# GpSimd's tap sums on VectorE, and another order of steps at the two ends of the attention

## The reference

```python
n = layernorm(x)                               # per token, 1024 channels
c = conv1d(n, conv_w, width 3) + conv_b        # 1024 -> 768 = q | k | v, 256 each
# blocks of 128 tokens, 16 heads of 64, causal inside a block
qh, kh, vh = q@wq + bq, k@wk + bk, v@wv + bv
p = softmax(where(causal, qh @ kh.T / 8, -1e9))
o = (p @ vh) @ wo + bo                         # 1024 -> 256
x1 = x + o @ proj_w + proj_b                   # 256 -> 1024
f = layernorm(x1)
y = f @ W_base.T + b_base                      # 1024 -> 1024
# 4 active experts of rank 8, gate = softmax(log prior + router logits)
out = x1 + y + sum_e 2 * gate_e * (f @ A_e.T) @ B_e.T
```

## Time and profile before

| | |
|---|---|
| median of 3 runs | 793.99 us (793.89 to 794.37) |
| the profiled execution | 794.1 us, of which 792.3 from the first to the last instruction |
| mean granted TensorE clock | 0.997 |
| TensorE busy | 767.2 us (97%) |
| VectorE busy | 516.3 us (65%) |
| ScalarE busy | 384.1 us (48%) |
| GpSimd busy | 203.1 us (26%) |

### The profile page before, as it was taken

How to read it: one execution, slowest core, us unless ns; L and a number is a source line. 1 busy time by engine, 2 the same in 40 slices (tenths; PEclk the granted TensorE clock), 3 DMA queues, 4 the chain that set the end, 5 groups by cost and what they waited for, 6 DMA issues and landing times.

```text
span 792.3 us, 14391 instructions
## 1 busy us (share of the span) xinstructions
PE 767.2 (97%) x5182; PEld 693.0 (87%) x5182; DVE 516.3 (65%) x1478; ACT 384.1 (48%) x1052; POOL 203.1 (26%) x192
## 2 busy tenths in 40 slices
PE   4999999999999999999999999999999999999996
PEld 3898888778778889989999989999889999999996
DVE  6999994778878756444444445545686766667652
ACT  5953442334333887676767676767851101111010
POOL 2400102222222235253534334352401111111100
PEclk9999999999999999999999999999999999999998
DMA  8746834534446230403063332102253534435301
GB/s 327 283 133 165 269 104 148 182 116 148 140 165 239 87 122 1 141 8 109 40 233 127 99 111 90 59 29 81 91 151 133 160 108 132 144 96 160 102 33 54
DMA packets 49435, 101.39 MB, mean 128 GB/s; under 512 B 10195, under 2 KB 26451, under 8 KB 48084
## 3 DMA queue, kind: packets, MB, share of 16 engines
q1 hardware_dynamic: 47060, 92.08, 35.3%
q0 software_dynamic: 2304, 8.39, 2.6%
HBM read 73.97 MB, written 26.08 MB: 126 GB/s over the span
## 4 chain that ended last, share of the span: by engine, by line
PE 69%; DVE 20%; ACT 5%; issue 2%; POOL 2%; DMA 0%; DVEq 0%; ACTq 0%; POOLq 0%
PE net_psum L63 17%; PE net_psum L65 17%; PE net_psum L64 17%; PE net_psum L1389 4%; PE net_psum L1412 4%; PE net_psum L1400 4%; DVE x_lo L950 2%; PE net_psum L1442 2%; PE net_psum L1443 2%; PE net_psum L1444 2%; POOL raw L520 1%; DVE raw L957 1%; ACT pr L682 1%; DVE ua L912 1%; DVE raw L958 1%
## 5 line engine op out<-in xcount | busy, mean ns | idle before, releaser
L63 PE MATMUL net_psum<-fw_hi,xT_hi 128*128 128x354 f32 (+1 forms) x384 | 127.2, 331 | 0.4 <-DVE fw_lo L1191 0.4
L64 PE MATMUL net_psum<-fw_lo,xT_hi 128*128 128x354 f32 (+1 forms) x384 | 124.2, 324 | 0.0
L65 PE MATMUL net_psum<-fw_hi,xT_lo 128*128 128x354 f32 (+1 forms) x384 | 124.2, 323 | 0.0
L546 POOL TENSOR_TENSOR pr<-pr,rrec 128x512 f32<-128x512 f32 x64 | 68.5, 1071 | 207.2 <-DVE rrec L1029 204.2
L682 ACT ACTIVATE pr<-pr,negmax 128x128 f32<-128x128 f32 x256 | 99.1, 395 | 1.0 <-DVE negmax L1021 1.0
L1327 PE MATMUL net_psum<-ua,wa 128*128 128x256 f32 x384 | 83.8, 379 | 0.5 <-DVE ua L915 0.5
L1021 DVE CUSTOM_DVE_ANT_0 pr<-net_psum,mask 128x128 f32<-128x128 f32 x256 | 57.1, 286 | 37.7 <-PE net_psum L1389 37.4
L1327 PEld LDWEIGHTS net_psum<-ua,wa 128*128 128x128 f32 x384 | 72.6, 190 | 10.3 <-issue 0.7
L63 PE MATMUL net_psum<-x_hi,w_hi 128*128 128x512 f32 x192 | 76.7, 400 | 1.7 <-DVE w_lo L964 1.5
L520 POOL TENSOR_TENSOR raw<-raw 128x512 f32<-128x512 f32 x24 | 36.8, 1536 | 161.2 <-ACT raw L631 161.2
L64 PE MATMUL net_psum<-x_lo,w_hi 128*128 128x512 f32 x192 | 76.0, 396 | 0.0
(11 more groups left out here) (191 smaller groups left out, 1813.9 us busy)
## 6 DMA issues: line engine op xcount, KB each, us to landing
wa<-in_conv_w SPq DMA_DIRECT2D x24, 512.0 KB, 4.0
raw<-in_conv_w SPq DMA_DIRECT2D x24, 384.0 KB, 3.8
xn<-in_x SPq DMA_DIRECT2D x16, 512.0 KB, 10.4
xr<-in_x SPq DMA_DIRECT2D x8, 1024.0 KB, 5.0
x_scratch<-xr SPq DMA_DIRECT2D x8, 1024.0 KB, 4.3
x1t<-x_scratch SPq DMA_DIRECT2D x16, 512.0 KB, 3.9
out<-y POOLq DMA_DIRECT2D x16, 512.0 KB, 4.9
x1g<-x_scratch SPq DMA_DIRECT2D x56, 128.0 KB, 3.2
```

Of the source, the lines that this page charges most:

```text
L63: pe.matmul(out, w_hi, x_hi, start=first, stop=False)
L64: pe.matmul(out, w_hi, x_lo, start=False, stop=False)
L65: return pe.matmul(out, w_lo, x_hi, start=False, stop=last)
L546: pool.tensor_tensor(pr[:, jj % 4], pr[:, jj % 4], rrec[:, jj % 4].unsqueeze(2).to_broadcast([P, UN, P]), ALU.mult).then_inc(s["p_ready"], 1)
```

## The change

Seven edits, on VectorE, ScalarE, GpSimd and TensorE:

1. `POOL_SUMS = 2`: GpSimd adds the scaled taps for units 0 and 1 only; for the other 22 VectorE does it, ahead of its two mixes, and waits for pre_ready itself.
2. `ends` of a block moves from the block's second slot to its third, but for the last block but one.
3. `low_weight(0)` goes ahead of the last two low parts of the input.
4. In double steps 2, 3 and 4 the queries and keys of the odd pair are copied out by VectorE (`queries_keys`, new) instead of ScalarE.
5. wo_lo (`low_heads`) goes from the ends of steps 2 and 3 to the end of step 1 and into step 4.
6. In step 32 TensorE's second projection unit goes behind the output sums; on VectorE one fw_lo (`low_dense(3)`) goes behind the masking, and both reciprocals ahead of the second addition.
7. The second half of tile 1's transposes uses bank 3 instead of 7, and waits for the pT copies instead of the last addition to x.

```diff
@@ -104,2 +104,3 @@
     FILL = 18
+    POOL_SUMS = 2
     EARLY = 5
@@ -261,3 +262,3 @@
         gp = psum[:, 0, 0:2 * TG].rearrange("p (g v) -> p g v", g=TG)
-        tp = ((psum[:, 0], psum[:, 6]),) + ((psum[:, 0], psum[:, 7]),)
+        tp = ((psum[:, 0], psum[:, 6]),) + ((psum[:, 0], psum[:, 3]),)
         yp = (tuple(psum[:, b] for b in (1, 2, 4)), tuple(psum[:, b] for b in (5, 6, 3)))
@@ -559,3 +560,3 @@
                 power(1, j)
-            for k in range(NK):
+            for k in range(POOL_SUMS):
                 mix(k)
@@ -735,4 +736,2 @@
                         queries_keys(2 * D)
-                    if D in (2, 3, 4) and h == 1:
-                        queries_keys(2 * D + 1)
                     if pair_of(D - SC) and (D, h) != (ND, 0):
@@ -955,2 +954,5 @@
                 tap = r[:, 0:1].to_broadcast([P, 2, 2, P])
+                if k >= POOL_SUMS:
+                    dve.wait_ge(s["pre_ready"], k + 1)
+                    dve.tensor_tensor(r[:, 2:5:2], r[:, 1:4:2], r[:, 2:5:2], ALU.add).then_inc(s["ef_ready"], 1)
                 dve.wait_ge(s["ef_ready"], k + 1)
@@ -1004,2 +1006,3 @@
                     sums(m, 0, TOK // P).then_inc(s["add_step"], 1)
+                if m >= 0 and k % NP4 == (1 if m == LAST - 1 else 2):
                     dve.wait_ge(s["add_step"], m + 1)
@@ -1043,2 +1046,11 @@
 
+            def queries_keys(J):
+                i = J % NP
+                dve.wait_ge(s["qk_done"], J + 1)
+                wait(dve, s["sc_done"], J - 1)
+                dve.wait_ge(s["qk_ready"], J)
+                for k, t in enumerate((qf, kf)):
+                    c = dve.tensor_scalar(t[:, J % 2], qk_acc(J)[:, k], bqk_c[:, k, i:i + 1], None, ALU.add)
+                c.then_inc(s["qk_ready"], 1)
+
             def unit_out(D, k):
@@ -1083,11 +1095,12 @@
                     low_dense(D - (ND - 3))
-                unit_out(D, 0)
                 if D == ND:
-                    reciprocals(2 * (D - SC))
-                    unit_out(D, 1)
-                    reciprocals(2 * (D - SC) + 1)
-                else:
-                    for jj in pair_of(D - SC):
-                        reciprocals(jj)
-                    unit_out(D, 1)
+                    low_dense(3)
+                if D == 4:
+                    low_heads(1)
+                unit_out(D, 0)
+                if D in (2, 3, 4):
+                    queries_keys(2 * D + 1)
+                for jj in pair_of(D - SC):
+                    reciprocals(jj)
+                unit_out(D, 1)
                 if D == 1:
@@ -1095,8 +1108,5 @@
                     last_sums(2)
+                    low_heads(0)
                 if D == 2:
                     last_sums(3).then_inc(s["cy_ready"], 1)
-                if D in (2, 3):
-                    k = D - 2
-                    dve.wait_ge(s["wo_hi_ready"], k + 1)
-                    dve.tensor_tensor(wo_lo[:, 4 * k:4 * k + 4], wo_raw[:, 4 * k:4 * k + 4], wo_hi[:, 4 * k:4 * k + 4], ALU.subtract).then_inc(s["wo_lo_ready"], 1)
                 if D in (5, 6):
@@ -1105,2 +1115,7 @@
 
+            def low_heads(k):
+                h = slice(4 * k, 4 * k + 4)
+                dve.wait_ge(s["wo_hi_ready"], k + 1)
+                dve.tensor_tensor(wo_lo[:, h], wo_raw[:, h], wo_hi[:, h], ALU.subtract).then_inc(s["wo_lo_ready"], 1)
+
             def tile_statistics(t):
@@ -1225,5 +1240,6 @@
                 inputs(c)
+                if c == DC - 1:
+                    low_weight(0)
                 if c:
                     low_input(c - 1)
-            low_weight(0)
             low_input(DC - 1)
@@ -1258,3 +1274,2 @@
             low_dense(2)
-            low_dense(3)
             attention_pair(ND)
@@ -1464,5 +1479,8 @@
                     queries_keys(2 * D + 1)
-                run_unit(D, 1)
+                if D != ND:
+                    run_unit(D, 1)
                 for jj in pair_of(D - PV):
                     output_sums(jj)
+                if D == ND:
+                    run_unit(D, 1)
 
@@ -1474,3 +1492,3 @@
                     if t == 1 and h == 1:
-                        pe.wait_ge(s["x1_ready"], YT * NG)
+                        pe.wait_ge(s["pT_ready"], NJ)
                     wait(pe, s["xT_lo_ready"], 2 * (t - 1) + h + 1)
```

More of the change, by code:

```diff
@@ L1083, in attention_pair @@
                     low_dense(D - (ND - 3))
+                if D == ND:
+                    low_dense(3)
+                if D == 4:
+                    low_heads(1)
                 unit_out(D, 0)
-                if D == ND:
-                    reciprocals(2 * (D - SC))
-                    unit_out(D, 1)
-                    reciprocals(2 * (D - SC) + 1)
-                else:
-                    for jj in pair_of(D - SC):
-                        reciprocals(jj)
-                    unit_out(D, 1)
+                if D in (2, 3, 4):
[3 more added lines that the diff above has]
+                unit_out(D, 1)
                 if D == 1:
```

## The result

The changed kernel takes 786.35 us (median of 4 runs, 786.11 to 786.48), the kernel before in the runs beside it 794.0 (793.89 to 794.37, 4 runs): a ratio of 0.9904, 95% interval 0.9892 to 0.9916. The forecast was 787.1 in 785.4 to 789.8. The profiled execution took 786.38 with a span of 784.5, against 794.1 and 792.3.

What follows compares the result with a forecast made beforehand. TensorE was taken to set the pace, so moved work counts only through its waits. Convolution 2.5, attention's start 2.3, attention's end 1.7 and last transposes 0.4 sum to 6.9 off 794.1; the median lies 0.1 lower: 787.1 us, range 785.4 to 789.8.

Steps and rivals of the forecast that it cites:

- Convolution: Convolution units: w_lo waits, lost overlap and the late first split matmul all go, for -2.5 us.
- ends go to the next slot: Convolution on VectorE: ends (two steps) leave the slot of the sums, so w_lo no longer comes at the last moment.
- VectorE no longer meets GpSimd: Convolution: w_lo, up to 1.98 against 1.22, and the first of the ends, 1.66 against 0.69, are no longer lengthened.
- The 0.69 a sum: Convolution: a tap sum on VectorE costs 0.69 us, like the mixes, adding some 14 us of VectorE time.
- The 2.7 us of cover: Convolution: the next w_lo is done about 2.9 us into a unit and needed at 5.6, leaving 2.7 spare.
- Rival 4: Convolution: slower because sums on VectorE cost GpSimd's median of 1.6 us, making VectorE the bound; 800.8 us, 4%.
- SP's cover of 6.9 us: SP's queue in the convolution: tap loads behind later stores have 6.9 us and land in 2.8 to 6.6; barely holds.
- Attention's start: Double steps at the attention's start: moving qf, kf and wo_lo shortens output-sum and turns waits, for -2.3 us.
- The new wait: Scores of the eighth head pair: TensorE waits 0.6 us for keys behind oT_lo and both c_lo steps on VectorE.
- second turns: Attention's start, second wait at the transposes of the softmax products: 0.3 us left of 1.1.
- Rival 1: Attention's start: no new wait at the scores, so the whole 3.7 goes; 785.7 us, 13%.
- Attention's end: Projection's second part: its wait for pT is covered by output sums put ahead and an earlier copy, for -1.7 us.

Runs made afterwards that it cites:

- order alone: Kernel before with one edit, the first w_lo ahead of the low part of the seventh input on VectorE: 793.18 us, 1.02 below before.
- one more step: Changed kernel with VectorE doing the first mix step twice in 22 slots: 796.61 us, 2.4 above the kernel before.
- a kernel without it: Changed kernel with VectorE's two c_lo steps moved behind the eighth head pair's queries and keys: 786.17 us, 7.70 below before.
- two more steps: Changed kernel with VectorE doing the first mix step three times in 22 slots: 809.90 us.

## Why the prediction was right, and where it was not

The forecast lay 0.75 above the measured time, and the convolution's term makes most of that. The kinds of wait that were to go went, and the one that was to come came.

- **Convolution, -2.5 against -3.1: the term was mis-sized, and one of its two reasons was wrong.** The size: I counted a wait as its entry and 0.16 of lost overlap. The traces show one thing more: behind each of the four inner late starts the next start comes 0.34 later, not 0.233, so 0.1 each. The first start came 1.14 earlier, of which the start behind it gives back 0.08, so 1.05 and not 0.86. The reason "ends go to the next slot" is worth nothing beside the sums (790.88 with it, 790.92 without) and costs 1.3 alone. The sums' move carries all of it, the first start included, which I had explained by order; order alone would have brought that start too (1.02). Of the inner losses, "VectorE no longer meets GpSimd" is one cause, and the mix that no longer waits for GpSimd's sum is another, which I had left out.
- **The 0.69 a sum** held (0.685), and with it the sign. The 2.7 us of cover did not: one more step of 0.7 us a slot already loses 10. Rival 4's sum, at 1.4 a sum, gives 17.3 + 5.6 = 22.9, so 0.5 x 5 + 2 x 2.3 - 4.4 = 2.7 above before, and 2.4 was measured; at 2.1 it gives 16.7, and 15.7 was measured. That the sizes agree is in part luck: with one more step VectorE, the bound in that sum, idled 12 of 112 us, and late taps are in the measured times but not in that sum.
- **SP's cover of 6.9 us** "holds, barely": ScalarE waited 0.9 us for taps that landed after up to 7.1, the sign I had named against me, at no cost to TensorE. The load is issued 1.6 into the unit and not 1.1 (178.08; the unit's first matmul starts at 176.48), which leaves 6.4 of the 6.9. With the sums alone, the ends in their old slot, ScalarE waited for no tap load at all.
- **Attention's start**: 2.36 for 2.3. The new wait came by the steps as written. c_lo began at 273.34, which is 276.45 with the 3.11 of the convolution added (forecast 276.5); the pair took 0.78 from start to start (275.08 to 275.86; forecast 0.79); the entry is 0.57 for 0.6. By the starts it costs more, 0.84, of which 0.11 comes behind the late start. What was wrong is the count of the second turns: I left 0.3 there beside the kf wait, but the one covers the other, and a turns entry comes out only when kf is removed. GpSimd's pair of products is back at 2.04 from 3.02, as the term had it, and at 2.99 with wo_lo's old places. Turns still slip without an entry: eight of them take 1.31, 1.19 and 1.15 in the three double steps, where undisturbed ones take 1.09, 0.4 together. That is 1.2 left for the 1.4 of the forecast; 3.7 less 2.36 would be 1.3.
- **Rival 1** (no new wait, 785.7) is refuted twice over: the wait came, and a kernel without it is no faster.
- **Attention's end** 1.75 for 1.7, and the transposes 0.45 for 0.4: the waits went as written. Undoing both of TensorE's edits gives back 1.38 of the first and all of the second. One step holds only in that order: the "addition that nothing awaits yet" is awaited, for 1.10, where the output sums do not stand ahead of it.

## What to carry to other kernels

Ahead of moving work within an engine's order, look for steps of the same shape that take 1.7 us in some places and 0.7 in others: what runs beside them there may be much of the loss, and an order that only shifts them may make it worse. A new wait in the trace is not yet a loss, if the wait behind it ends at the same time without it. A reserve read from one engine's slot is not spare when a store and a load queued behind it wait for the last step of that slot: add a known step and see where the time starts to rise.

## What the runs showed of the hardware that was not expected

After the wait of 2.58 us at 197.34 above, starts came 0.43 apart instead of 0.233 for seven matmuls, some 1.6 us in all. The windows of that run (columns as above) show the granted clock at 0.53, near the lower level of 1.2 GHz, and then back:

```profile
198.00:201.40 3.40, 3.40 (x10) 2.68 (x9) 3.37 (x6) 1.43 (x3) 0.00 (x0) 0.53 0.36 118
201.40:205.00 3.60, 3.60 (x17) 2.92 (x16) 3.53 (x6) 2.05 (x2) 0.00 (x0) 1.00 0.00 0
```

With two more steps it came once as well, behind a late start at 204.13, but not behind this one, whose wait was longer:

```profile
176.00 0.50 PE L63 MATMUL net_psum<-x_hi,w_hi 128*128 128x512 f32 x1 [2.86 <-DVE w_lo L969]
```

So in two traces one wait of 2.6 to 2.9 us cost some 1.6 us more, and the runs do not tell when. The medians do not show it: with one more step, an execution at a mean granted clock of 0.999 took 796.72, and those at 0.996 took 796.12 to 797.47.
